# Edge maxima paced by the kind of mix step; rows to ScalarE, a shorter root, a bias by TensorE and one comparison in the last layer of a graph transformer kernel

## What is computed

```python
xn = layernorm(x)
x = x + gnn(xn, src, dst) + mix(xn)          # three graph attention layers; random-feature attention
x = x + ffn(layernorm(x))                    # routed experts

# gnn, per layer and head (3 x 4 heads of 192)
e = leaky_relu(as_n[src] + ad_n[dst]); m = segment_max(e, dst); p = exp(e - m[dst])
out = segment_sum(p / segment_sum(p, dst)[dst] * h[src], dst)

# mix, 12 heads of 64, 256 random features: exp(dash - diag - max) for k and q
# ffn
probs  = softmax(xf @ switch_w + switch_b)   # 8 experts
prob_max, routes = max(probs), argmax(probs)
rank   = position of a node among those of its expert, by falling prob_max, ties by index
keep   = rank < 195
out    = where(keep, expert[routes](xf), xf) * prob_max
```

## Time and profile before

| | |
|---|---|
| Median of 3 runs (lowest to highest) | 1721.52 us (1719.59 to 1725.29) |
| The profiled execution | 1720.55 us, span 1718.8 us |
| TensorE busy | 1582.5 us, 92% |
| VectorE busy | 1135.0 us, 66% |
| ScalarE busy | 680.6 us, 40% |
| GpSimd busy | 412.0 us, 24% |

### The profile page before, as it was taken

One profiled execution on the slowest core, in us unless ns is written; L12 is line 12 of the kernel. 1 busy time (PEld: TensorE's weight loads), 2 busy tenths in 40 slices (PEclk: granted clock), 3 DMA queues, 4 the chain that ended last, 5 costly groups with the idle time before them and its releaser, 6 DMA issues.

```text
span 1718.8 us, 25251 instructions
## 1 busy us (share of the span) xinstructions
PE 1582.5 (92%) x9809; PEld 1196.0 (70%) x9809; DVE 1135.0 (66%) x2618; ACT 680.6 (40%) x1359; POOL 412.0 (24%) x251
## 2 busy tenths in 40 slices
PE   3979999999989889999999999998999999986987
PEld 2556666555655568887888888888888976666664
DVE  6777664114466989898988697668765833785223
ACT  4421001122232466667767664336534521441110
POOL 3788888888400000000000000000000000002331
PEclk9999999999999999999999999999999999996999
DMA  9335535454752422223420264336312224645951
GB/s 360 83 60 118 119 77 118 61 92 74 198 178 85 143 76 84 88 80 102 134 81 28 64 191 144 125 108 202 131 47 79 88 83 146 220 180 201 315 160 50
DMA packets 194889, 213.67 MB, mean 124 GB/s; under 512 B 81359, under 2 KB 149597, under 8 KB 194770
## 3 DMA queue, kind: packets, MB, share of 16 engines
q1 hardware_dynamic: 118146, 187.01, 33.0%
q0 software_dynamic: 75760, 22.70, 8.3%
q10 hardware_dynamic: 864, 2.36, 0.4%
HBM read 144.74 MB, written 68.40 MB: 124 GB/s over the span
## 4 chain that ended last, share of the span: by engine, by line
PE 53%; POOL 16%; DVE 13%; DMA 7%; issue 6%; ACT 4%; SPq 0%; POOLq 0%; ACTq 0%; DVEq 0%
PE bank L1073 20%; POOL table L2117 16%; PE bank L902 6%; PE bank L904 6%; PE bank L903 6%; DMA table<-amount,place 4%; PE bank L1243 4%; PE bank L1231 3%; PE bank L1127 3%; PE bank L1099 2%; DVE junk L1478 2%; PE bank L1142 1%; DVE eb L1513 1%; PE bank L1112 1%; DVE eb L1522 1%
## 5 line engine op out<-in xcount | busy, mean ns | idle before, releaser
L1073 PE MATMUL bank<-hb,eb 128*128 128x193 f32 (+3 forms) x2400 | 417.7, 331 | 12.7 <-ACT node L1920 7.6
L1073 PEld LDWEIGHTS bank<-hb,eb 128*128 128x128 f32 (+3 forms) x2400 | 400.3, 190 | 23.3 <-issue 10.3
L2117 POOL DMA_INDIRECT table<-amount,place x170 | 346.9, 2040 | 73.3 <-issue 49.1
L2123 POOL IOTA iota8i<- 128x8 int32 x1 | 0.1, 140 | 952.7 <-DMA node_rows<-node 952.7
L1513 DVE SCALAR_TENSOR_TENSOR eb<-shift_b,as_low,shift_b 128x640 f32<-128x640 f32 (+1 forms) x240 | 196.5, 861 | 0.3 <-PE bank L1073 0.2
L1906 ACT ACTIVATE eb<-eb,asd 128x640 f32<-128x640 f32 (+1 forms) x240 | 181.4, 812 | 28.7 <-DVE eb L1513 28.7
L1478 DVE CUSTOM_DVE_ANT_0 junk<-ab,absent 128x1250 bf16<-128x1250 f32 x120 | 174.2, 1452 | 1.1
L1522 DVE SCALAR_TENSOR_TENSOR eb<-eb,count 128x1280 f32<-128x1280 f32 (+1 forms) x120 | 174.6, 1455 | 0.0
L902 PE MATMUL bank<-wg_hi,x1T_hi 128*128 128x384 bf16 (+3 forms) x360 | 118.6, 329 | 0.3 <-DVE x1T_lo L1345 0.3
L903 PE MATMUL bank<-wg_lo,x1T_hi 128*128 128x384 bf16 (+3 forms) x360 | 118.6, 329 | 0.0
L904 PE MATMUL bank<-wg_hi,x1T_lo 128*128 128x384 bf16 (+3 forms) x360 | 118.6, 329 | 0.0
(11 more groups left out here) (290 smaller groups left out, 3011.2 us busy)
## 6 DMA issues: line engine op xcount, KB each, us to landing
w<-in_w SPq DMA_DIRECT2D x16, 1152.0 KB, 10.1
shift_b<-shift_rows SPq DMA_DIRECT2D x24, 625.0 KB, 5.7
h_rows<-h_row SPq DMA_DIRECT2D x27, 388.0 KB
hb<-h_rows SPq DMA_DIRECT2D x12, 873.0 KB
ar<-node_rows SPq DMA_DIRECT2D x27, 384.0 KB
table<-zero POOLq DMA_DIRECT2D x3, 3054.0 KB, 19.0
tab<-table SPq DMA_DIRECT2D x27, 312.5 KB, 3.7
qk_rows<-qk_row SPq DMA_DIRECT2D x12, 625.0 KB
```

The source lines that it names most:

```text
L1073: ins = T.matmul(bank[w // 2][0:M, c0:c0 + GC + 1], p[0:K, u, w * P:w * P + M], hv[0:K, t, 0:GC + 1], start=opens and u == 0 and w % 2 == ...
L2117: G.indirect_dma_start(tables[i], bass.IndirectOffsetOnAxis(place[:, c:c + 1], axis=0), amount16[:, c:c + 1], None, compute_op=ALU.add).th ...
```

## The change

- The rate of the edge maxima depends on the kind of the newest mix step: 0.5 a turn while it is a q step, else 1.1 (before: 0.8 always). The mix steps note their kind in the set `done`.
- `new_norm`: the variance is negated where the epsilon is added; ScalarE's root gets a scale that makes up for it and for a factor ROOT, so that VectorE issues three small instructions behind the reciprocal (two for the Newton step, one for the bias, minus mean times r) where it issued four. The normalised rows are then made by ScalarE (Identity with scale and bias) instead of VectorE.
- The routing bias is added by one more product on TensorE (a row of ones by the bias row) into the same bank, and `logits` of VectorE goes; `route` reads the bank itself.
- `rank` compares all columns up to the tile's end with "at least" in one instruction, where it compared the earlier tiles' columns with "at least" and its own tile's with "more"; `uncount`, minus one on and behind the diagonal, takes back what is counted too many among the equal ones.

```diff
--- before.py
+++ after.py
@@ -58,7 +58,8 @@
 ITEMS = 2 * SPLITS
 HROWS = D // 2
 WEIGHT_SETS = 5
-ROUTE_STEPS, RANK_STEPS = 7, 4
+ROUTE_STEPS, NORM_STEPS, RANK_STEPS = 6, 5, 4
+ROOT = 2.0 ** (2 / 3)
 OUT_ROWS = 4
 PARTS = ((0, 105), (105, 195))
 WIDEST = PARTS[0][1]
@@ -66,7 +67,7 @@
 NOWHERE = 4096.0
 
 COUNTS_AT = 17
-COUNT_RATE, EARLY_EDGE_RATE, FIRST_EDGE_RATE, EDGE_RATE, ATTENTION_RATE = 0.5, 0.75, 1.1, 0.8, (0.4, 0.5)
+COUNT_RATE, EARLY_EDGE_RATE, FIRST_EDGE_RATE, EDGE_RATE, ATTENTION_RATE = 0.5, 0.75, 1.1, (1.1, 0.5), (0.4, 0.5)
 
 
 def rows(t):
@@ -287,7 +288,7 @@
                       lambda: "projected" in done and "first_shift" in done)
     yield "head_in", 0
     yield from spread(edges, lambda: FIRST_EDGE_RATE, lambda: "first_pair" in done)
-    yield from paced((attention_steps(done), lambda: ATTENTION_RATE["mixed" in done]), (edges, EDGE_RATE))
+    yield from paced((attention_steps(done), lambda: ATTENTION_RATE["mixed" in done]), (edges, lambda: EDGE_RATE["q" in done]))
 
 
 def edge_steps(done):
@@ -347,6 +348,8 @@
         pair, kind, t = order[n]
         if n == 2 * NT:
             done.add("first_pair")
+        done.discard("q")
+        done.add(kind)
         if "open" not in done:
             yield "warm_mix", 2
         if kind == "k" and t == 5 and pair + 1 < PAIRS:
@@ -614,7 +617,7 @@
         share16 = put("share16", [P, 3, NT], BF16)
         at_logits = cursor[0]
         lg, ex = put("lg", [P, NT, EXPERTS]), put("ex", [P, NT, EXPERTS])
-        earlier = put("earlier", [P, P])
+        uncount = put("uncount", [P, P])
         stats3 = put("stats3", [P, NT, 16])
         b2r = [put("b2r0", [128, D])]
         iota_row = put("iota_row", [P, WIDEST], BF16)
@@ -725,7 +728,7 @@
         pr, ro = put("pr", [P, N]), put("ro", [P, N])
         mate, won = put("mate", [P, N], BF16), put("won", [P, N], BF16)
         even, win = put("even", [P, P], BF16), put("win", [P, P], BF16)
-        cnt = put("cnt", [P, 3, NT])
+        cnt = put("cnt", [P, 2, NT])
         signs = put("signs", [P, 2], BF16)
         assert cursor[0] <= after_features
         cursor[0] = r_d
@@ -1174,9 +1177,9 @@
                 pe.wait_ge("f_hi", 2 * t + 2)
                 pe.wait_ge("rank_rows", t)
                 for k in range(KD):
-                    ins = T.matmul(bank[2][0:R, 0:EXPERTS], fT[t % 2][:, k, 0:R], sw[:, k, :], start=k == 0,
-                                   stop=k == KD - 1)
-                ins.then_inc(sem["logit_mm"], 1)
+                    T.matmul(bank[2][0:R, 0:EXPERTS], fT[t % 2][:, k, 0:R], sw[:, k, :], start=k == 0, stop=False)
+                T.matmul(bank[2][0:R, 0:EXPERTS], ones[0:1, 0:R], sbias[0:1, :], start=False,
+                         stop=True).then_inc(sem["logit_mm"], 1)
 
             def rank_turn(t):
                 R = rows(t)
@@ -1627,48 +1630,36 @@
 
             def new_norm(t):
                 R = rows(t)
-                v, r, u = (stats3[:, t, i:i + 1] for i in (13, 14, 15))
-                n = 6 * t
+                mean, v, r, u = (stats3[:, t, i:i + 1] for i in (12, 13, 14, 15))
+                n = NORM_STEPS * t
                 ve.wait_ge("x2", 3 * (t + 1))
-                V.tensor_scalar(v, v, LN_EPS, None, ALU.add).then_inc(sem["x2_norm"], 1)
+                V.tensor_scalar(v, v, LN_EPS, -1.0, ALU.add, ALU.mult).then_inc(sem["x2_norm"], 1)
+
                 ve.wait_ge("x2_root", t + 1)
                 V.reciprocal(r, u).then_inc(sem["x2_norm"], 1)
                 ve.wait_ge("x2_norm", n + 2)
-                V.tensor_tensor(u, v, r, ALU.mult).then_inc(sem["x2_norm"], 1)
+                V.tensor_scalar(u, v, r, r, ALU.mult, ALU.mult).then_inc(sem["x2_norm"], 1)
                 ve.wait_ge("x2_norm", n + 3)
-                V.tensor_tensor(u, u, r, ALU.mult).then_inc(sem["x2_norm"], 1)
+                V.tensor_scalar(r, u, 3.0 / ROOT, r, ALU.add, ALU.mult).then_inc(sem["x2_norm"], 1)
                 ve.wait_ge("x2_norm", n + 4)
-                V.tensor_scalar(u, u, -0.5, 1.5, ALU.mult, ALU.add).then_inc(sem["x2_norm"], 1)
-                ve.wait_ge("x2_norm", n + 5)
-                V.tensor_tensor(r, r, u, ALU.mult).then_inc(sem["x2_norm"], 1)
-                ve.wait_ge("x2_norm", n + 6)
-                V.tensor_scalar(xf[0:R, t, :], x2[0:R, t, :], stats3[0:R, t, 12:13], stats3[0:R, t, 14:15],
-                                ALU.subtract, ALU.mult).then_inc(sem["xf_ready"], 1)
-
-            def logits(t):
-                R = rows(t)
+                V.tensor_scalar(v, mean, -1.0, r, ALU.mult, ALU.mult).then_inc(sem["x2_norm"], 1)
+
+            def route(t):
+                R = rows(t)
+                n = ROUTE_STEPS * t
+                lt, et, out = lg[0:R, t, :], ex[0:R, t, :], bank[2][0:R, 0:EXPERTS]
+                most, prob, which, total = (pm[0:R, i, t:t + 1] for i in (0, 1, 2, 7))
                 ve.wait_ge("logit_mm", t + 1)
-                ve.wait_ge("switch_in", 32)
+                V.tensor_reduce(most, out, AX.X, ALU.max).then_inc(sem["route_v"], 1)
                 ve.wait_ge("iota_f", 3)
-                V.tensor_tensor(lg[0:R, t, :], bank[2][0:R, 0:EXPERTS], sbias[0:R, :],
-                                ALU.add).then_inc(sem["route_v"], 1)
-
-            def route(t):
-                R = rows(t)
-                n = ROUTE_STEPS * t
-                lt, et = lg[0:R, t, :], ex[0:R, t, :]
-                most, prob, which, total = (pm[0:R, i, t:t + 1] for i in (0, 1, 2, 7))
                 ve.wait_ge("route_v", n + 1)
-                V.tensor_reduce(most, lt, AX.X, ALU.max).then_inc(sem["route_v"], 1)
-                ve.wait_ge("iota_f", 2)
-                ve.wait_ge("route_v", n + 2)
-                V.tensor_scalar(et, lt, most, None, ALU.subtract).then_inc(sem["route_v"], 1)
-                V.scalar_tensor_tensor(lt, lt, most, iota8[0:R, :], ALU.is_lt, ALU.max).then_inc(sem["route_v"], 1)
-                ve.wait_ge("route_v", n + 4)
+                V.tensor_scalar(et, out, most, None, ALU.subtract).then_inc(sem["route_v"], 1)
+                V.scalar_tensor_tensor(lt, out, most, iota8[0:R, :], ALU.is_lt, ALU.max).then_inc(sem["route_v"], 1)
+                ve.wait_ge("route_v", n + 3)
                 V.tensor_reduce(which, lt, AX.X, ALU.min).then_inc(sem["route_v"], 1)
                 ve.wait_ge("route_exp", t + 1)
                 V.tensor_reduce(total, et, AX.X, ALU.add).then_inc(sem["route_v"], 1)
-                ve.wait_ge("route_v", n + 6)
+                ve.wait_ge("route_v", n + 5)
                 V.reciprocal(prob, total).then_inc(sem["route_v"], 1)
 
             def rank(t):
@@ -1686,17 +1677,14 @@
                 ve.wait_ge("beat", t - 1)
                 V.tensor_scalar(mate[0:R, 0:hi], ro[0:R, 0:hi], which, None, ALU.is_equal).then_inc(sem["ranks"], 1)
                 ve.wait_ge("ranks", n + 1)
-                for p0, p1, op, j in ((0, lo, ALU.is_ge, 0), (lo, hi, ALU.is_gt, 1)):
-                    if p1 > p0:
-                        ins = V.scalar_tensor_tensor(won[0:R, p0:p1], pr[0:R, p0:p1], prob, mate[0:R, p0:p1], op,
-                                                     ALU.mult, accum_out=cnt[0:R, j, t:t + 1])
-                ins.then_inc(sem["ranks"], 1)
+                V.scalar_tensor_tensor(won[0:R, 0:hi], pr[0:R, 0:hi], prob, mate[0:R, 0:hi], ALU.is_ge, ALU.mult,
+                                       accum_out=cnt[0:R, 0, t:t + 1]).then_inc(sem["ranks"], 1)
                 V.scalar_tensor_tensor(even[0:R, 0:R], pr[0:R, lo:hi], prob, mate[0:R, lo:hi], ALU.is_equal,
                                        ALU.mult).then_inc(sem["ranks"], 1)
                 ve.wait_ge("pool_set", 10)
                 ve.wait_ge("ranks", n + 3)
-                V.scalar_tensor_tensor(win[0:R, 0:R], even[0:R, 0:R], 1.0, earlier[0:R, 0:R], ALU.mult, ALU.mult,
-                                       accum_out=cnt[0:R, 2, t:t + 1]).then_inc(sem["ranks"], 1)
+                V.scalar_tensor_tensor(win[0:R, 0:R], even[0:R, 0:R], 1.0, uncount[0:R, 0:R], ALU.mult, ALU.mult,
+                                       accum_out=cnt[0:R, 1, t:t + 1]).then_inc(sem["ranks"], 1)
 
             def ranked(_):
                 ve.wait_ge("ranks", RANK_STEPS * NT + 1)
@@ -1789,7 +1777,7 @@
                         k_top=k_top, top_max=top_max, top_turn=top_turn, top_spread=top_spread, count=count_, absent=absent_, edge_max=edge_max, shifts=shifts, weigh=weigh,
                         finish=finish, q_exp=q_exp, divide=divide, out_split=out_split,
                         x_bias=x_bias, row_split=row_split, row_add=row_add,
-                        expert_setup=expert_setup, new_x=new_x, new_norm=new_norm, logits=logits, route=route,
+                        expert_setup=expert_setup, new_x=new_x, new_norm=new_norm, route=route,
                         rank=rank, ranked=ranked, mapped=mapped, own=own_, slots_turn=slots_turn,
                         expert_out=expert_out)
```

(21 more changed lines are left out.)

2 lines of the change are left out of this document (removed).

## The result

| | before | changed |
|---|---|---|
| median of 20 runs | 1721.81 us | 1725.97 us |
| ratio | | 1.0022, 95% interval 1.0013 to 1.0031 |
| span of the profiled execution | 1718.8 us | 1721.8 us |

A forecast was written before the change was run, and what follows sets the result against it. In the mix TensorE and VectorE were taken to hold each other up by turns, in the last layer one cross-engine tile loop to set the pace. Mix -9 and last layer +6 gave -3 us: 1719 us, range 1707 to 1730.

The forecast's parts named there:

- The last layer: Last layer's tiles, about 1440 to 1560 us: moving rows to ScalarE exposes a table load; +6 us, bounds +2 and +10.
- 0.87 us on a tile: Last layer: each probability comes 0.87 us later as the exp's table load waits for the rows; nine tiles, +7.8 us.
- R+0.78: Last layer: forecast start of the rows on ScalarE, counted from R, the reciprocal of the root on VectorE.
- the tile with the late rows: Last layer: one tile where a transfer of rows holds TensorE back 2.47 us; it may swallow part of one 0.87.
- Rival 3: Last layer: exp's table load stands ahead of the rows, so VectorE's saving counts; -8 there, 1704 us in all; chance 0.07.
- rival 4: Last layer: more than the load stands between rows and exp on ScalarE, up to 0.96 us nine times; 1728 us; chance 0.04.
- The mix: Interleaved attention, graph items and edge maxima, about 630 to 986 us: new edge rates shorten waits for exps; -9 us.
- After: k 2.71, q 2.68: Mix: forecast VectorE time in us per k and q step under the new rates, against 2.29 and 3.09 before.
- rival 2: Mix gains nothing, VectorE late at every k phase's end, first q steps wait; 0 to +2, 1729 us; chance 0.22.
- VectorE's slack at the q phases: Mix: VectorE's 4.77 us idle waiting for TensorE at a q phase's start, forecast to be nearly gone.
- the 38%: Mix: item and edge maximum coincide 38% less in a q step; of 18.1 us waits for exps, that saves 7 us.
- The ceiling of 22 us: Mix, best case: all TensorE idle goes, 4.8 us in each of four middle pairs and some 3 in the last.

## Why the prediction was wrong

- **The last layer was right,** in mechanism and nearly in size. +6 us was forecast, bounds +2 and +10; +8 was measured alone. I put 0.87 us on a tile, it was 1.10. The difference is a term that I priced from the wrong row: of the three small steps behind the reciprocal, the first reads two scalars a partition from memory and takes 0.27 us, the other two read one and take 0.21, where I took the 0.16 of the steps before, so that the rows start at R+1.01 and not at R+0.78. That the sum came out near has some luck in it: in the profiles eight tiles lost 11.1 us, above the bound of +10, and the tile with the late rows, of which I had said that it may swallow a part of one 0.87, gave 3.2 us back. Rival 3 (the load ahead of the rows) did not come about; nor did rival 4: in the timeline of the tile the load begins 0.01 us after the rows' end and the exp 0.02 us after the load's end, so nothing but the load stands there.
- **The mix is where it failed.** -9 us was forecast, -3.6 measured. The step that failed is the one that treated blank steps as k steps: "After: k 2.71, q 2.68" was worked out for k and q, and nothing for the blank ones, so that what the maxima cost there stood in the sum as nothing. The products there and the next pair's sums over features share one bank (`bank[7]`), and each waits for VectorE's reciprocal and ScalarE's division of the one before; at 1.1 maxima a turn the reciprocal stood behind three of them, and TensorE's waits for the division rose from 3.8 to 6.7 us. My rival 2 had VectorE late at the end of every k phase, and TensorE held up in the first q steps; it was late in the blank steps, and TensorE was held up by another instruction. Nor did VectorE's slack at the q phases go, as I had said it would: its waits for TensorE ahead of the query maxima are 28.5 us where they were 30.1.
- **The gain was priced from the wrong row.** The waits of the weight loads for exps fell as I said, to 9.9 us where I had 11. But the 38% were taken of their 18.1 us. What the transposes themselves cost TensorE was 11.0 us, and it fell by 5.8, the last pair's share included, where my sum has 9. 5.8 saved and 2.9 lost leave -2.9, near the -3.6 measured. An edge maximum was put too low as well: 1.38 us from one pair of starts, where three in a row start 1.46 to 1.51 us apart.
- **The price of a wait.** In the sum a wait cost its own length. In the changed kernel the two longest were each followed by a stretch at half clock, which about doubled them; slow blank steps gave 7 us, not 3, and nearly all of the 7 is clock.
- **The ceiling of 22 us was too high.** With half of each maximum gone the kernel gains 14.6 us, 9.5 of them at full clock. What idle is left ends with ScalarE; how much of it VectorE still causes isn't parted.
- **The chances.** Slower on the whole had 0.23 for more than 0.3%; the 0.22% is within the range and within the 0.3% that I called no change, but twenty runs do tell it from none, and with the sign that I did not forecast.

## What to carry to other kernels

Before work moves to ScalarE, write down the order of its functions in one turn and mark where the table changes: an instruction put between the last use of one table and the first of the next takes the load out of cover, here 1.28 us a tile for 0.6 us of VectorE saved. When the rate of a background track is set by phase, work out every phase by itself, the short ones with a serial chain above all. A wait is to be priced from the row of the engine that does the work, not from that of its weight loads. A loop made faster is to be asked which transfer it will now meet. And where the effect is under 1%, the granted clock of every run tells how much of a gain is work and how much is clock.

## What was not expected of the hardware

- A wait of TensorE of 2 to 3 us in the middle of dense work went with a stretch at 1.2 GHz: 2.89 us and then 6.8 us at half clock, 2.08 us and 3.4 us, in the changed kernel and in the kernel with the rates alone alike; with the waits gone, the stretches were gone too. Stretches of that length also occur elsewhere, so that each is not shown to have such a cause. What is shown over all runs is the sum: beside the kernel before, the clock took 1.2 us more with the rates alone and 5.7 less with slow blank steps.
- A tensor_scalar of one column took 0.27 us with two scalars from memory (the same one, read twice), 0.21 with a number and one scalar from memory, and 0.15 with numbers alone (L1633 and L1641 of the kernel before).
- A product over one row (the bias, 1x8 into 128 rows) took its two records 0.31 us on TensorE's queue (1511.28 to 1511.59). No run takes it out alone, so that it is hidden isn't shown; with it in place a tile's period was down to 9.3 us.
